# A graph kernel's second aggregation: projection before the row table instead of after the sums, sums scaled straight into the residual

## The reference, cut to what matters

```python
x = x + _L0_gnn_ref(_layernorm(x), ...)
x = x + _L0_ffn_ref(_layernorm(x)[None], ...)[0]    # 8 experts, top 2: each node gets two rows, weighted by gates
x = x + _L1_gnn_ref(_layernorm(x), L1_gnn_W, L1_gnn_b, edge_index)
x = x + _L1_ffn_ref(_layernorm(x)[None], ...)[0]    # slice attention

def _L1_gnn_ref(x, W, b, edge_index):
    src, tgt = edge_index
    xt = x @ W.T + b
    out = segment_sum(xt[src], tgt, num_segments=3125)
    deg = segment_sum(ones, tgt, num_segments=3125)
    return out / (deg + 1.0)[:, None]
```

## Time and profile before

| | us |
|---|---|
| median of 3 runs (lowest, highest) | 2016.87 (2011.6, 2018.67) |
| the profiled execution's own time | 2011.72 |
| its span in the trace | 2010.0 |
| combine stage, walk, node stage in the trace | 1229 to 1282, 1282.5 to 1788, 1788 to 1817.4 |

### The profile page before, as it was taken

One profiled execution on the slowest core, in us unless ns is written; L12 is line 12 of the kernel. 1 busy time (PEld: TensorE's weight loads), 2 busy tenths in 40 slices (PEclk: granted clock), 3 DMA queues, 4 the chain that ended last, 5 costly groups with the idle time before them and its releaser, 6 DMA issues. The chain is left out here.

```text
span 2010.0 us, 22839 instructions
## 1 busy us (share of the span) xinstructions
PE 1349.0 (67%) x6532; PEld 1131.2 (56%) x6532; DVE 876.4 (44%) x1747; ACT 570.3 (28%) x1256; POOL 1099.5 (55%) x1086
## 2 busy tenths in 40 slices
PE   2535666666665365699999993165656665687978
PEld 2324545444444255699999993144544454575757
DVE  7425544444443677533333334522222222247943
ACT  2133433333333024233333331222222222232310
POOL 4376777777774500575222570377777777723520
PEclk6756877877787575799999997578878788788989
DMA  6484898888886503242111025533333333310002
GB/s 143 117 248 148 299 307 278 283 283 286 278 282 222 143 0 99 95 137 101 45 45 45 31 94 121 168 105 105 104 104 104 105 105 105 105 37 1 0 1 64
DMA packets 156802, 268.48 MB, mean 134 GB/s; under 512 B 26747, under 2 KB 119839, under 8 KB 155567
## 3 DMA queue, kind: packets, MB, share of 16 engines
q1 hardware_dynamic: 97027, 132.55, 20.8%
q0 software_dynamic: 46224, 123.97, 20.4%
q10 hardware_dynamic: 13438, 10.56, 2.3%
HBM read 169.82 MB, written 98.15 MB: 133 GB/s over the span
## 5 line engine op out<-in xcount | busy, mean ns | idle before, releaser
L1201 PE MATMUL bank<-sum_held,sum_hot 128*125 128x256 f32 x992 | 303.9, 476 | 252.1 <-ACT sum_held L1211 250.3
L1183 POOL DMA_INDIRECT sum_rows<-xn_tab,src_e x391 | 373.7, 956 | 172.8 <-issue 118.8
L1201 PEld LDWEIGHTS bank<-sum_held,sum_hot 128*125 128x125 f32 x992 | 236.2, 244 | 317.2 <-issue 257.1
L798 POOL DMA_INDIRECT gat_rows<-xh_tab,src_e x363 | 344.2, 948 | 115.9 <-issue 108.2
L871 PE MATMUL bank<-gat_rows,gat_same 128*128 128x264 f32 x784 | 266.9, 488 | 125.7 <-issue 125.7
L871 PEld LDWEIGHTS bank<-gat_rows,gat_same 128*128 128x128 f32 x784 | 179.2, 247 | 166.2 <-issue 132.0
L1211 ACT COPY sum_held<-sum_rows 128x1024 f32 x124 | 122.3, 1042 | 384.4 <-SPq L1174 372.1
L1879 PE MATMUL bank<-weights,e_xthigh 128*128 x896 | 219.2, 328 | 8.2 <-DVE e_xtlow L2004 5.4
L1231 DVE TENSOR_TENSOR sums<-sums,bank 125x256 f32 x124 | 52.1, 420 | 363.0 <-PE bank L1201 361.3
L915 ACT COPY gat_outs<-bank 128x528 f32<-128x528 f32 x196 | 117.5, 599 | 284.2 <-PE bank L871 283.8
L2009 DVE TENSOR_TENSOR e_h<-e_gated,bank 128x342 f32<-128x342 f32 x112 | 57.1, 510 | 261.0 <-ACT e_gated L1949 261.0
(11 more groups left out here) (499 smaller groups left out, 2375.9 us busy)
## 6 DMA issues: line engine op xcount, KB each, us to landing
parts<-gat_outs SPq DMA_DIRECT2D x27, 1904.0 KB, 8.1
staged<-w_tab SPq DMA_DIRECT2D x8, 2132.0 KB, 8.7
w_tab<-w_stage SPq DMA_DIRECT2D x16, 682.0 KB, 10.5
w_raw<-in_L_ffn_w_dram SPq DMA_DIRECT2D x16, 640.0 KB
gat_rows<-xh_tab,src_e POOLq DMA_INDIRECT x391, 4.0
sum_rows<-xn_tab,src_e POOLq DMA_INDIRECT x391, 2.7
w_tab<-w_stage SPq DMA_DIRECT2D x8, 768.0 KB, 10.6
w_raw<-in_L_ffn_w_dram SPq DMA_DIRECT2D x8, 682.0 KB, 11.5
```

What stands on the lines that cost most here:

```text
L798: pool.indirect_dma_start(out=rows[b % R][:, t, :], out_offset=None, in_=k.xh_tab, in_offset=bass.IndirectOffsetOnAxis(ap=k.src_e[:, b * S ...
L1183: pool.indirect_dma_start(out=rows[:, at // IP % (RING * GPAIRS), at % IP, :], out_offset=None, in_=k.xn_tab, in_offset=bass.IndirectOffse ...
L1201: m = nc.tensor.matmul(k.ps[s][0:P, 0:C], hot[g % 2][:, s, c, :], held[:, s, c, :], start=(c == 0), stop=(c == IP - 1))
```

## The change

The projection by W moves ahead of the table. In the combine stage W is centred (each row less its mean, which takes the place of subtracting the node's mean), turned on PE, and each node tile of `k.res` is transposed, copied, multiplied and scaled by its 1/deviation on ACT's way out of PSUM; `xn_tab` then holds projected rows. The item sums of the walk are scaled by 1/(deg+1) and added to `k.res` itself, and DVE takes `bn_stats` of the tile after every item (the last one of a tile is the one that counts). The node stage is gone. The bias is added to `k.res` at the walk's start in 25 instructions on end (`Prep.begin`), where it was one between items. Batches of the ring have 4 tiles, not 8, in 16 slots, not 8 (the same bytes); `LAND` is 1; the two empty items are gone. SP issues both choices' loads, turn by turn.

```diff
-GB = 8
+GB = 4
-RING = 8
+RING = 16
-LAND = 2
-AHEAD = 3
+LAND = 1
+AHEAD = 6
@@ class Prep @@
-    STEPS, FIRST, EVERY = 14, 2, 2
+    STEPS, FIRST, EVERY, SKIP = 12, 2, 2, 2
+    def begin(self, dve):
+        k, v, me = self.k, self.k.nc.vector, self.k.steps["dve"]
+        me(dve, v.tensor_scalar(self.inv[:, :], k.deg[:, :], 1.0, None, ALU.add))
+        me(dve, v.reciprocal(self.inv[:, :], self.inv[:, :]))
+        me(dve, v.tensor_tensor(self.part[:, :], self.inv[:, :], k.deg[:, :], ALU.mult))
+        dve.wait_ge(self.bias_in, 16)
+        for t in range(NT):
+            m = v.scalar_tensor_tensor(out=k.res[:, t, :], in0=self.bias[:, :], scalar=self.part[:, t:t + 1], in1=k.res[:, t, :], op0=ALU.mult, op1=ALU.add)
+        me(dve, m)
@@ sum_phase @@
             for s in k.retired:
                 pool.sem_clear(s)
+            me, diag = st["pool"], k.att["diag"]
+            me(pool, nc.gpsimd.memset(diag[:, :], 0.0))
...
-                for s in range(IB):
+                for s in range(min(IB, ITEMS - g * IB)):
...
-                    into = tile_of(k.sums, node)
-                    v.tensor_tensor(into, into, k.ps[s][0:P, 0:C], ALU.add).then_inc(added, 1)
+                    into = tile_of(k.res, node)
+                    v.scalar_tensor_tensor(out=into, in0=k.ps[s][0:P, 0:C], scalar=prep.inv[:, bass.ds(node, 1)], in1=into, op0=ALU.mult, op1=ALU.add).then_inc(added, 1)
+                    dve.wait_ge(added, n + 1 + IB)
+                    v.bn_stats(tile_of(k.stats, node), into)
...
-            me(dve, v.memset(k.sums[:, :, :], 0.0))
+            prep.begin(dve)
@@ experts_phase, SP @@
+            sp.wait_ge(k.w_split, NE)
+            sp.dma_start(gw, k.a["L1_gnn_W"].rearrange("(a p) c -> p a c", p=128)).then_inc(gw_in, 16)
             sp.wait_ge(y_out, 16 * NI)
             for g in range(GROUPS):
                 move(sp, ys[:, 0, g * TB:(g + 1) * TB, :], y_rows[:, 0, g * TB:(g + 1) * TB, :], ys_in[g])
+                move(sp, ys[:, 1, g * TB:(g + 1) * TB, :], y_rows[:, 1, g * TB:(g + 1) * TB, :], seconds_in[g])
@@ experts_phase, PE @@
+            for t in range(NT + 1):
+                if t < NT:
+                    pe.wait_ge(rows_made, t + 1)
+                    if t >= XR:
+                        pe.wait_ge(yt_kept, t - XR + 1)
+                    for c in range(2):
+                        m = nc.tensor.transpose(YT[t % XR][:, c * P:(c + 1) * P], k.res[:, t, c * 128:(c + 1) * 128], k.ident[0:P, 0:P])
+                    m.then_inc(y_turned, 1)
+                if t:
+                    pe.wait_ge(yt_kept, t)
+                    if t > len(XT):
+                        pe.wait_ge(xt_scaled, t - len(XT))
+                    for c in range(2):
+                        m = nc.tensor.matmul(XT[(t - 1) % len(XT)], yt[:, (t - 1) % XR, c, :], gwt[:, c, :], start=(c == 0), stop=(c == 1))
+                    m.then_inc(multiplied, 1)
@@ experts_phase, ACT @@
-                move(act, ys[:, 1, g * TB:(g + 1) * TB, :], y_rows[:, 1, g * TB:(g + 1) * TB, :], ys_in[g])
...
+                for t in tiles:
+                    act.wait_ge(y_turned, t + 1)
...
+                    nc.scalar.copy(yt[:, t % XR, :, :].rearrange("p a n -> p (a n)"), YT[t % XR][:, 0:2 * P]).then_inc(yt_kept, 1)
+                act.wait_ge(deviations, g + 1)
+                nc.scalar.activation(k.rstd[:, g * TB:(g + 1) * TB], spread[:, g * TB:(g + 1) * TB], ACT.Sqrt, bias=eps[:, 0:1], scale=1.0 / C).then_inc(roots, 1)
+                act.wait_ge(scaled, g + 1)
+                for t in tiles:
+                    act.wait_ge(multiplied, t + 1)
+                    nc.scalar.activation(xn[:, t, :], XT[t % len(XT)], ACT.Identity, scale=k.rstd[:, t:t + 1]).then_inc(xt_scaled, 1)
@@ experts_phase, DVE @@
+            def invert(g):
+                rstd = k.rstd[:, g * TB:(g + 1) * TB]
+                dve.wait_ge(roots, g + 1)
+                v.reciprocal(rstd, rstd).then_inc(scaled, 1)
...
+                if g:
+                    invert(g - 1)
+                dve.wait_ge(seconds_in[g], 32)
@@ build @@
-            gnn_node_phase(k)
```

More of the change, by code:

```diff
@@ L1066, in on_tensor @@
         half = j % 2
[L1067 to L1073, removed]
+        if j > self.SKIP:
+            pe.wait_ge(self.kept, j - self.SKIP)
+        if j < 6:
             pe.wait_ge(wx_in, 48)
@@ L1205, in _ @@
         def _(act):
-            for n in range(ISLOTS):
+            for n in range(ITEMS):
                 pair = ring_pair(act, n)
@@ L1801, in experts_phase @@
         PRODUCTS = ((0, 0), (0, 1), (1, 0))
+        YT, XT = k.ps[0:XR], [bank[0:P, 0:C] for bank in k.ps[XR:8]]
         HH = [HB[a + 1] - HB[a] for a in range(2)]
@@ L1985, in _ @@
             steps(start, item, finish)
-            act.wait_ge(y_out, 16 * NI)
+            act.wait_ge(gw_turned, 1)
+            nc.scalar.copy(gwt.rearrange("p a c -> p (a c)"), YT[0][:, 0:2 * C]).then_inc(gw_ready, 1)
             for g in range(GROUPS):
-                move(act, ys[:, 1, g * TB:(g + 1) * TB, :], y_rows[:, 1, g * TB:(g + 1) * TB, :], ys_in[g])
-            for half in range(2):
-                norm_roots(k, act, deviations, roots, slice(*HALVES[half]), half + 1)
-                act.wait_ge(scaled, half + 1)
-                for t in range(*BY_ACT[half]):
-                    nc.scalar.activation(xn[:, t, :], k.res[:, t, :], ACT.Identity, bias=shift[:, t:t + 1], scale=k.rstd[:, t:t + 1]).then_inc(by_act, 1)
+                tiles = range(g * TB, (g + 1) * TB)
+                for t in tiles:
+                    act.wait_ge(y_turned, t + 1)
+                    if t >= XR:
+                        act.wait_ge(multiplied, t - XR + 1)
+                    nc.scalar.copy(yt[:, t % XR, :, :].rearrange("p a n -> p (a n)"), YT[t % XR][:, 0:2 * P]).then_inc(yt_kept, 1)
[5 more added lines that the diff above has]
+                    nc.scalar.activation(xn[:, t, :], XT[t % len(XT)], ACT.Identity, scale=k.rstd[:, t:t + 1]).then_inc(xt_scaled, 1)
         @block.vector
@@ L2038, in _ @@
             me = k.steps["dve"]
-            for g in range(GROUPS):
-                dve.wait_ge(ys_in[g], 64)
-                for j in range(2):
-                    for t in range(g * TB, (g + 1) * TB):
-                        m = v.scalar_tensor_tensor(out=k.res[:, t, :], in0=ys[:, j, t, :], scalar=k.gate[:, j, t:t + 1], in1=k.res[:, t, :], op0=ALU.mult, op1=ALU.add)
-                    me(dve, m)
-                for t in range(g * TB, (g + 1) * TB):
-                    v.bn_stats(k.stats[:, t, :], k.res[:, t, :])
-                half = 0 if (g + 1) * TB == HALVES[0][1] else 1 if g == GROUPS - 1 else None
-                if half is not None:
-                    tiles = slice(*HALVES[half])
-                    norm_factors(k, dve, deviations, roots, tiles, half + 1)
-                    v.scalar_tensor_tensor(out=shift[:, tiles], in0=k.mv[:, tiles, 0], scalar=-1.0, in1=k.rstd[:, tiles], op0=ALU.mult, op1=ALU.mult).then_inc(scaled, 1)
@@ new lines, in _ @@
+            v.memset(eps[:, :], EPS)
+            dve.wait_ge(gw_in, 16)
+            me(dve, v.tensor_reduce(gw_mean[:, :], gw, AX, ALU.add))
+            me(dve, v.tensor_scalar(gw_mean[:, :], gw_mean[:, :], 1.0 / C, None, ALU.mult))
+            for a in range(2):
+                m = v.tensor_scalar(gw[:, a, :], gw[:, a, :], gw_mean[:, a:a + 1], None, ALU.subtract)
+            m.then_inc(gw_centred, 1)
+            def invert(g):
+                rstd = k.rstd[:, g * TB:(g + 1) * TB]
+                dve.wait_ge(roots, g + 1)
+                v.reciprocal(rstd, rstd).then_inc(scaled, 1)
@@ L2117, in attention_phase @@
+            invert(GROUPS - 1)
 def attention_phase(k):
```

120 lines of the change are left out of this document (39 added, 81 removed).

## The result

The changed kernel takes 1988.72 us (median of 4 runs, 1984.28 to 1993.71); the kernel before, run beside it, 2014.23 (2005.87 to 2018.67, 4 runs). The ratio is **0.9889, 95% interval 0.9858 to 0.992**: 22 us faster. The forecast was 1985.9 (1977 to 1999). The profiled execution took 1993.71, the slowest of the four, with a span of 1992.0: 18.0 less than the 2010.0 of before, where the sum had said 31.0.

| term | forecast | in the trace |
|---|---|---|
| node stage gone | -29.2 | -29.2 |
| combine stage, from first load's issue to first gather | +3.4 | 56.07 for 52.85: +3.2 |
| walk, first to last gather's start | +0.4 | 496.76 for 491.56: +5.2 |
| last gather's start to next stage | -5.6 | 11.10 for 14.09: -3.0 |
| attention stage | 0 | 197.6 for 192.6: +5.0 |

What follows compares the result with a forecast made beforehand. The walk, a quarter of the span, was taken as bound by POOL's gather issuing, the node stage by PE. Terms -29.2 + 0.4 - 5.6 + 3.4 = -31.0 from the 2016.87 median gave 1985.9 us, 8-in-10 range 1977 to 1999.

Steps and rivals of the forecast that it cites:

- Node stage: Stage between walk and attention stage: goes whole, -29.2 us, its work moved into the combine stage and the walk.
- Combine stage: From first loads to first gather: new loop over five groups starts late and runs longer, +3.4 us, bounds 1.4 to about 7.
- The path that sets the loop: Combine stage: ACT's scalings, PE's transposes with ACT's copies, then root and reciprocal, 7.5 us a group against DVE's own 7.0.
- rival 1: Combine stage: PE falls back to 1.2 GHz between groups, +11 us in four turns, time 1997; chance 0.17.
- Rival 2: Combine stage loads: SP's queue alone moves half, loads end at 1287, time 2001; chance 0.05.
- Finer batches: Walk: POOL has 82 waits where it had 41, costing 0 to 1.4 us, taken as +0.4.
- so that costs nothing: Walk's start: bias additions together, about 10.4 us, delay only DVE's marks and adds; the ring takes 80 us of gathers first.
- rival 4: Walk: DVE's added 52 us hold up POOL's gathers one for one, sum +21, time 2038; chance 0.03.
- Walk's end: Last gather's start to next stage: one item left instead of four, 8.5 us for 14.1, -5.6.
- the low-clock case: Walk's end with PE at low clock for the last item: 9.3 us including 0.29 for the barrier.
- Rival 3: Walk's end: POOL's 80 clears and three memsets after the last gather end the walk, +7 us, time 1993; chance 0.06.
- a colder PE at its start: Attention stage: named as a way to be wrong, the stage taking back what was won; no size given.

## Why the prediction was right, and where it was not

- **Node stage: right.** Its 29.2 us went whole; neither walk nor combine stage had to pay for its work beyond what was counted.
- **Combine stage: right, +3.2 for +3.4, with errors that cancelled.** The path that sets the loop is the one that was named, over ACT and PE; it took 6.9 us a turn for 7.5 (from first to fifth copy 4.3 for 4.7, root and hand-overs 0.5 for 0.7), and DVE's own work 6.5 for 7.0. Against these 1.7 us in three turns stands the first turn of 8.6, since the second group was in part at half clock too (rival 1 for one group of five). The second half of group 0 landed 1.2 us later than I took, counted from the first load's issue, but the first root was only 0.3 late. That the sum comes out within 0.2 is luck. Why the second group lost the clock is open: it did behind a pause of PE of 1.86 us here, and with the bias additions spread it kept it behind a pause of the same 1.86. What the prediction cites of the Trainium skill (TensorE: Matmul & The Clock Gate, section HAM oscillation) tells of waits longer than this loop's pause, so it does not say that each group here begins cold, and three of five did not. Rival 2 fell: the loads of one queue kept up, and undoing it cost 6.9 us.
- **Finer batches: right.** Below 0.4; no difference from first to last gather.
- **Walk's steady part: the step "so that costs nothing" of the bias additions failed.** I looked only for who waits on DVE for data, and put rival 4 on the instructions that were added. The work that hurt was the one that stayed as much and was put together: 5.8 us (shown by spreading it, and by doubling it). The Trainium skill (SBUF — State Buffer, the trap in which DVE blocks a DMA) describes a near relative: GpSimd is kept from writing descriptors while VectorE runs an instruction of a mode that takes two ports, such as an fp32 copy inside SBUF. Whether these additions are of that kind, and what holds the gather inside POOL, no row shows. The traces show only when: in an unbroken run of 25 two-input additions out of and into SBUF, and not beside the same instruction in fours (1.25 us at most), the statistics, or the long memset.
- **Walk's end: -3.0 for -5.6; the term lacked POOL's drain.** DVE's path alone came to 9.6 us with the barrier, where 8.5 was taken and 9.3 was the low-clock case. The drain cost a further 1.5 us in this trace (1794.42 for 1792.65 + 0.29) and 3.3 where PE was at full clock. The finer batches released the last item but one earlier, as planned, which brought DVE 2 us forward, and made the drain 3.3 us longer, which took it back. Rival 3 had the right engine and the wrong cause: the clears are not in it, and that they stand ahead of the last gathers could be seen in the trace of before.
- **Attention stage: +5.0 where the sum had nothing.** I named a colder PE at its start; the start was alike (granted clock 0.77 over its first 30 us in both), and the middle was not. Twelve traces have this stage without added matmuls, and its time goes with its mean granted clock: 191.2 us at 0.93, 192.6 at 0.92 (three traces), 194.0 at 0.91, 197.6 at 0.89 (five), 198.8 at 0.88 and 201.9 at 0.86. The 192.6 have 13 us at half clock in the middle, the 197.6 have 27. With PE's pauses filled it was 188.8. The change does not rule out the good value, since two kernels that contain it had 192.6 as before. I take it for a spread of every such kernel; but each was profiled once, so that one kernel shows both values is not shown, nor what decides it.

In the median the change gave 22 to 26 us of the 31.0, so the saving was forecast 5 to 9 us too high. The forecast time was only 2.8 off, and part of that is luck: it started from 2016.87 us, and the kernel before, run beside the changed one, had 2014.23. From there the same sum gives 1983.2, 5.5 off. The sum of the traces, 18.0, is lower than the median's because the profiled executions happened to lie 5.0 us above the one median and 2.5 below the other.

## What to carry to other kernels

When work moves on an engine that waits for nobody, look at what it will run beside, unbroken: a run of cheap DVE instructions in front of a walk paced by POOL's gathers was not free here (5.8 us), and spreading it was. At a stage's end read the queues' drains, not only the last instruction of each engine; POOL's can outlast all of them. And compare stages between traces with their granted clock, before a difference of a few us in an untouched stage is put down to a change.

## What I had not expected of the hardware

- A gather that started 4.0 to 4.8 us into a run of 25 of DVE's SBUF-to-SBUF additions stood until 0.8 us after it (6.81, 6.82 and 6.83 us in four kernels, 6.03 for the one that started at 4.8), while gathers in the first 4 us went through at 0.95 to 1.28.
- The drain of POOL's queue behind its last visible work took 3.2 to 9.1 us, the same to the nanosecond in the nine kernels with 16 slots of 4 (9109) and in the two with 8 of 4 (3229).
- One DMA issue held ACT's queue for 5.4 us while the loads before it were under way, and the copies behind it waited.
- Seventeen matmuls that nobody reads, in three pauses, raised PE's mean granted clock in the middle from 0.89 or 0.77 to 1.00; the stage took 188.8 us for 192.6 or 197.6 (one trace).
